# A selective-scan stage: GpSimd takes 8 of the 24 products with B instead of 7, two in one instruction

## The reference, cut to what matters

```python
def step(h_prev, t):
    x_t, dt_t, B_t, C_t = t
    dA = jnp.exp(dt_t[..., None] * A)
    dBx = (dt_t * x_t)[..., None] * B_t[:, :, None, :]
    h = dA * h_prev + dBx
    y = jnp.einsum('bkdn,bkn->bkd', h, C_t)
    return (h, y)
```

## Time and profile before

| | us |
|---|---|
| median of 3 runs | 22312.98 (22303.36 to 22334.86) |
| the profiled execution, its own time | 22314.07 |
| span of its trace | 22312.3 |
| VectorE busy in the span | 19495.2 (87%) |
| GpSimd busy in the span | 16107.3 (72%) |
| TensorE busy in the span | 16801.2 (75%) |

### The profile page before, as it was taken

One profiled execution on the slowest core, in us unless ns is written; L12 is line 12 of the kernel. 1 busy time (PEld: TensorE's weight loads), 2 busy tenths in 40 slices (PEclk: granted clock), 3 DMA queues, 4 the chain that ended last, 5 costly groups with the idle time before them and its releaser, 6 DMA issues. The chain is left out here.

```text
span 22312.3 us, 287094 instructions
## 1 busy us (share of the span) xinstructions
PE 16801.2 (75%) x84632; PEld 5876.1 (26%) x84632; DVE 19495.2 (87%) x21108; ACT 9584.4 (43%) x14631; POOL 16107.3 (72%) x5892
## 2 busy tenths in 40 slices
PE   8999999989997777777777777777777777777731
PEld 5555555552221111111111111111111111111111
DVE  5555555559998999999999999999999999999976
ACT  3433433337774444444444444444444444444410
POOL 0000000006667999999999999999999999999977
PEclk9999999999997777777777777777777777766765
DMA  0000000016666666666666666666666666666666
GB/s 20 15 16 16 15 16 15 16 37 226 231 227 154 131 129 126 126 128 128 129 129 131 128 128 126 126 129 130 129 128 128 128 127 125 130 131 129 128 144 163
DMA packets 1129422, 2519.98 MB, mean 113 GB/s; under 512 B 247606, under 2 KB 448824, under 8 KB 1112960
## 3 DMA queue, kind: packets, MB, share of 16 engines
q1 hardware_dynamic: 1128320, 2508.11, 50.2%
HBM read 2000.43 MB, written 507.38 MB: 112 GB/s over the span
## 5 line engine op out<-in xcount | busy, mean ns | idle before, releaser
L1212 POOL TENSOR_TENSOR c_pr<-c_hs,c_c_u 128x1568 f32<-128x1568 f32 x3072 | 10794.1, 3525 | 546.5 <-DVE c_hs L1176 473.0
L1119 ACT ACTIVATE c_psum<-c_dt_u,c_a_neg 128x784 f32<-128x784 f32 x6144 | 5641.7, 918 | 8236.2 <-DVE c_hs L1176 8192.6
L1064 PE MATMUL c_psum<-c_pr,c_red 128*64 128x392 f32 x24576 | 7302.9, 713 | 2.7 <-POOL c_pr L1212 2.7
L1176 DVE TENSOR_TENSOR_SCAN c_hs<-c_psum,c_carry,c_dbx 128x784 f32<-128x784 f32 x3264 | 6347.1, 2025 | 0.0
L1053 PE MATMUL c_psum<-c_br_u,c_sel 48*128 48x512 bf16 (+1 forms) x8704 | 3008.3, 438 | 4148.5 <-DVE c_dbx L1156 4051.7
L1156 DVE TENSOR_TENSOR c_dbx<-c_u_u,c_psum 128x784 f32<-128x784 f32 x4352 | 4857.3, 1116 | 51.7 <-PE c_psum L1053 51.7
L195 POOL TENSOR_TENSOR a_xpb<-a_x_sb,a_pb_sb 98x768 f32<-98x768 f32 x128 | 231.5, 1809 | 4641.0 <-DVE a_x L283 4627.4
L1201 POOL TENSOR_TENSOR c_dbp<-c_u_u,c_bp_u 128x784 f32<-128x784 f32 x1792 | 3334.4, 1861 | 42.3 <-DMA c_c_u<-scr_bc 42.3
L1176 DVE TENSOR_TENSOR_SCAN c_hs<-c_psum,c_carry,c_dbp 128x784 f32<-128x784 f32 x1344 | 2734.2, 2034 | 0.0
L1053 PEld LDWEIGHTS c_psum<-c_br_u,c_sel 48*128 48x128 bf16 x8704 | 524.4, 101 | 8379.4 <-DVE c_dbx L1156 7925.3
L1064 PEld LDWEIGHTS c_psum<-c_pr,c_red 128*64 128x64 f32 x24576 | 1804.3, 178 | 3472.2 <-issue 3188.6
(11 more groups left out here) (117 smaller groups left out, 18555.2 us busy)
## 6 DMA issues: line engine op xcount, KB each, us to landing
c_c_u<-scr_bc SPq DMA_DIRECT2D x512, 1568.0 KB, 28.9
c_dt_u<-scr_dt SPq DMA_DIRECT2D x512, 588.0 KB, 7.4
c_u_u<-scr_u SPq DMA_DIRECT2D x512, 588.0 KB, 11.4
c_bp_u<-scr_bc SPq DMA_DIRECT2D x512, 588.0 KB, 22.2
scr_dt<-p_dt_o SPq DMA_DIRECT2D x384, 392.0 KB, 3.0
scr_u<-p_u_o SPq DMA_DIRECT2D x384, 392.0 KB, 2.4
scr_y<-c_y_sb SPq DMA_DIRECT2D x256, 294.0 KB, 17.8
d_yin<-scr_y SPq DMA_DIRECT2D x32, 2352.0 KB, 14.4
```

Source lines behind the costliest of these rows:

```text
L1064: mm = pe.matmul(Y(3 * w + q)[64 * h:64 * h + 64, :], red[:], pr[:, s % RP, HT * h:HT * h + HT], start=(p == 0 and opens(w)), stop=(p == N ...
L1119: nc.scalar.activation(dA(s), dt_u[:, d, s // NPR, :], ACT.Exp, scale=a_neg[:, k, s:s + 1]).then_inc(exp_done, 1)
L1176: nc.vector.tensor_tensor_scan(hs[:, s % RH, way], dA(s)[:, way], data, init, ALU.mult, ALU.add).then_inc(scan_done, 1)
L1212: nc.gpsimd.tensor_tensor(pr[:, s % RP:s % RP + 2, :], hs[:, s % RH:s % RH + 2, :], c_u[:, d, s % NPR:s % NPR + 2, :], ALU.mult).then_inc( ...
```

## The change

`POOL_STEPS` becomes (3, 5, 7, 11, 13, 15, 19, 23); VectorE's own steps are then 16. GpSimd forms its products with B two at a time, for the steps (3, 5), (7, 11), (13, 15) and (19, 23), with one instruction that writes both tiles of `dbp`. The pairs are issued behind the products with C that start at s = 20 (of the unit before), 0, 6 and 12. Where both steps are of one third, u is read twice by a broadcast; for (7, 11) two thirds of u are read, and the two rows of `bp_u` in reverse order. The wait is now for the scan that read the pair's second tile last.

```diff
-POOL_STEPS = (3, 7, 11, 13, 15, 19, 23)
+POOL_STEPS = (3, 5, 7, 11, 13, 15, 19, 23)
 DVE_STEPS = tuple(s for s in range(3 * NPR) if s not in POOL_STEPS)
@@
-            def times_b(b, w, i):
-
-                d, v, s = w % 2, WI * b + w, POOL_STEPS[i]
-                if i == 0:
+            def times_b(b, w, j):
+
+                d, v, i = w % 2, WI * b + w, 2 * j
+                s0, s1 = POOL_STEPS[i], POOL_STEPS[i + 1]
+                if j == 0:
                     pool.wait_ge(u_in[d], in_of(b, w))
                 if not (isinstance(v, int) and v == 0 and i < RG):
-                    bv, bs = (v, POOL_STEPS[i - RG]) if i >= RG else (v - 1, POOL_STEPS[i - RG])
+                    bv, bs = (v, POOL_STEPS[i + 1 - RG]) if i >= RG else (v - 1, POOL_STEPS[i + 1 - RG])
                     pool.wait_ge(scan_done, STEPS * bv + bs + 1)
-                nc.gpsimd.tensor_tensor(dbp[:, (len(POOL_STEPS) * w + i) % RG, :], u_u[:, d, s // NPR, :],
-                                        bp_u[:, d, POOL_PAIRS.index(s % NPR), :], ALU.mult).then_inc(bp_done, 1)
+                q0, q1 = s0 // NPR, s1 // NPR
+                p0, p1 = POOL_PAIRS.index(s0 % NPR), POOL_PAIRS.index(s1 % NPR)
+                u = u_u[:, d, q0:q0 + 1, :].to_broadcast([128, 2, CT]) if q0 == q1 else u_u[:, d, q0:q1 + 1, :]
+                rows = bp_u[:, d, p0:p1 + 1:p1 - p0, :] if p1 > p0 else bp_u[:, d, p0::p1 - p0, :]
+                nc.gpsimd.tensor_tensor(dbp[:, i % RG:i % RG + 2, :], u, rows, ALU.mult).then_inc(bp_done, 2)
@@
-                        if s + 7 in POOL_STEPS:
-                            times_b(b, w, POOL_STEPS.index(s + 7))
+                        if s + 7 in POOL_STEPS[2::2]:
+                            times_b(b, w, POOL_STEPS.index(s + 7) // 2)
```

## The result

The changed kernel takes 23379.76 us (median of 4 runs, 23368.41 to 23398.35) against 22308.17 us before (4 runs): a ratio of 1.0483, 95% interval 1.0467 to 1.0498. It is 4.8% slower. The profiled execution has a span of 23381.2 us, 1069 us above the one of before.

The account below looks back on a forecast made before the run. VectorE was taken to set the pace, GpSimd close behind. Losses less VectorE's saving gave +4.56 us for 192 units with carry and +4.76 for 64 without, +1181 on 22314: 23495 us, +5.3%, range 23345 to 23760.

Parts of the forecast that it names:

- The direction and the mechanism: Slower, at 93%: pairs wait for scans freeing their second tile, with products with C queued behind; +1181 us.
- the walk: GpSimd's queue followed through a unit: pairs (7, 11) and (13, 15) wait for scans 5 and 11; the others cost nothing.
- VectorE's saving: One product with B a unit, that of step 5, leaves VectorE: -0.86 us, 256 times, -220 us.
- The pair: GpSimd's instruction for two products with B: taken at 3.465 us, between 3.31 and 3.61.
- The chain: From the start of scan 5 to scan 8, and of 11 to 14: 9.25 us with carry, 9.17 without.
- The losses: Scans 5 to 8 and 11 to 14, beyond VectorE's unhindered time: 2.27 + 3.15 = 5.42 us a unit with carry.
- The waits expected: VectorE waiting for GpSimd's pairs and products some 1400 us; GpSimd idle about 5.9 us a unit, almost all ahead of two pairs.
- That GpSimd comes late enough to pay nothing: Rival, 5%: GpSimd reaches its two waits for scans after they are over; only VectorE's saving counts, 22094 us.
- That capacity sets the end: Rival, 3%: GpSimd keeps its 2.1 us of waits on top of its added work, 57.5 us a unit, 22574 us.
- That GpSimd holds VectorE up: Rival, 1%: VectorE could not read SBUF while GpSimd did; +90 us, 22400 us.
- long unbroken run: VectorE's recorded scan duration creeps from 1.87 to 2.07 us there at equal spacing; 1.87 was taken behind a stall.

Follow-up runs that it names:

- ring4: The changed kernel with four tiles in dbp instead of two, all else as it is: 22128.6 us, ratio 0.992 to the kernel before.
- half_pairs: The changed kernel with each pair instruction cut to the first 392 of 784 tokens, waits and order unchanged: 22557.53 us, ratio 1.0111 to the kernel before.
- singles8: The kernel before with step 5 also given to GpSimd, each product with B its own instruction, two tiles in dbp: 22193.32 us, ratio 0.995.

## Why the prediction was right

**The direction and the mechanism** hold at each step. But for the 13 waits ahead of scan 0 that were there before, VectorE waits only ahead of scans 7 and 8 and of 13 and 14, where the walk put the waits; GpSimd stands idle only ahead of the pairs (7, 11) and (13, 15). The other two pairs cost nothing. ring4 takes away the waits and nothing else, and 1250 us go.

**VectorE's saving** of 0.86 us a unit is real. It can't be seen in the changed kernel, but with the waits gone it is: ring4 lies 182 us below the kernel before. The full 220 aren't reached. The expectation of ring4 had a reason for that: in units without carry GpSimd needs 55.4 us and VectorE only 55.3 - 0.86 = 54.4. The trace shows another. VectorE never waits for GpSimd there. It waits for ScalarE's dA 29 times, 44.5 us in all, each time ahead of scan 19 in the first of two units without carry; the second takes 54.45 us every time, VectorE's own time. ScalarE in turn waits for a DMA, the store of `y_sb` to HBM, before it may write that tile again. ScalarE's waits for it in the stage, before and in ring4:

```profile
ACT c_y_sb L1109 <- DMA scr_y<-c_y_sb: 50.6, 27, 2.7
...
ACT c_y_sb L1109 <- DMA scr_y<-c_y_sb: 118.3, 29, 5.3
```

In the kernel before, these waits held up no scan. VectorE's waits grow from 23 us to 65, and the 42 are about what is missing (38). Why the store lands later against VectorE's work is not tested; in ring4 GpSimd ends the unit before it some 1.6 us later, and with it the loads start later that stand in SyncE's queue ahead of the store.

**The pair** was taken at 3.465 us, by the product with C, and takes 3.46 with the reversed rows (12022.21 to 12025.67) and 3.45 with the broadcast (12038.27 to 12041.72). Neither costs anything. The 3.40 worked out from the 2.6 cycles an element of the Trainium skill (GPSIMD Engine Reference, section 3.1) is a little under it.

**The chain was sized a little too long**, and this term is nearly all of the 115 us between the forecast 23495 and the measured 23380. It was put at 9.25 us and measures 9.06 and 9.07 (12020.22 to 12029.28, 12036.28 to 12045.35). The scan takes 1.84 instead of 1.87. GpSimd starts 12022.21 - 12022.06 = 0.15 us behind its end, not 0.20. VectorE starts 12029.28 behind a product that began at 12025.67 and lasts 3.50 as GpSimd's others do: 0.11 us, not the 0.20 borrowed from TensorE's start. The losses are then 9.06 - 6.98 = 2.08 and 9.07 - 6.10 = 2.97, so 5.05 us for 5.42 forecast. In units without carry the chain measures 9.01 and 9.00 instead of 9.17. For 256 units that is some 90 us. The unit comes out at 56.72 - 0.86 + 5.05 = 60.91, against 60.95 read. The other 25 us aren't traced one by one. No term of the chain was put too short, so the time lies only 35 us above the lower end of the range.

**The waits expected** were 1400 us for VectorE and 5.9 us a unit for GpSimd; they are 1233 (20 of them ahead of scan 0, as before) and 1328 / 256 = 5.2, smaller by the same shorter chain.

**The rivals.** That GpSimd comes late enough to pay nothing is refuted by its 3.28 and 2.20 us of idle time. That capacity sets the end is refuted by ring4 with the same load and half_pairs with less. That GpSimd holds VectorE up was put aside because both are busy at once; that is a weak reason, since an engine that is held up can be recorded as busy. The spacing decides: a scan takes 1.76 us with GpSimd idle beside it (12020.22 to 12021.98) and 1.76 beside a product with C (12025.74 to 12027.50). The rule of the Trainium skill (Perfetto Trace Analysis, Optimizing Scalar/DVE Operations), that moving work between the two might not help, is not what these instructions show: moving the eighth product gains 0.5% in singles8.

## What to carry to other kernels

Merging two instructions into one makes the new one wait for the later of their two free tiles: when pairing, double the ring with it, or look what stands behind the wait in that engine's queue. Price such a wait as a chain, from the scan that frees the tile to the last instruction that needed what is queued behind, less what the waiting engine can do meanwhile. Here the ring's two tiles turned a gain of 0.8% into a loss of 4.8%.

## What the runs showed that was not expected

The duration recorded for an instruction on VectorE is not what it takes of the engine. Scans with carry are recorded at 2.07 us in the earlier trace rows and at 1.84 in the changed kernel, and the product with B at 1.17 and at 0.94, while their spacing is the same in both, 1.76 and 0.86 us. Whoever adds up recorded durations finds VectorE's instructions faster by a tenth or more after the change, and they are not; the spacing is what the engine needs.

The prediction tied the longer duration to a long unbroken run. In the kernel before, the product with B is recorded at 0.95 us in the first 20 us behind a stall and at 1.01 on average from 120 to 250 us behind it. But ring4 shows that a long run alone does not make it grow. There VectorE runs over 400 us at a time without a recorded wait, and the product with B is recorded at 0.94 us all the same:

```profile
L1156 DVE TENSOR_TENSOR c_dbx<-c_u_u,c_psum 128x784 f32<-128x784 f32 x4096 | 3857.2, 942 | 51.4 <-PE c_psum L1053 51.4
```

What makes it grow in the kernel before stays open.

Two waits on one queue did not add up. Moving both pairs gave 661 us, moving the first alone 120.
